# Both attentions of a decoder kernel: scores formed twice, by rows for the maximum and transposed for the exponential

## The chip, the cores and the metric

One program on one NeuronCore of a Trainium2 chip. It runs eight stages one after the other. The metric is the device time of the whole program in microseconds (us); a change under 0.2% is within what repeated measurements of one kernel spread.

## The reference, cut to what matters

Batch 32, sequence 128, width 128, everything float32. The two stages in question compute, for 16 heads of width 8:

```
stage 1 (attn0):  xn = layer_norm(x);  q, k, v = xn @ Wqkv + b;  q, k = rope(q), rope(k)
                  p = softmax(q k^T / sqrt(8) + causal mask);  y = x + (p v) @ Wo + b
stage 4 (attn1):  xn = rms_norm(x);    q, k, v = xn @ wq, wk, wv      (no bias, no rope, no mask)
                  p = softmax(q k^T / sqrt(8));  y = x + (p v) @ wo
```

The other stages are a gelu network, a retention layer, a mixture of experts, a bidirectional Mamba block, a cross attention and a quantized network. They are not changed.

## The kernel before, in words

Each stage is a block of five instruction streams (PE, DVE, ACT, POOL, SP) that run in their own order and meet at semaphores. `attention(..., rope)` at L250 serves both stages; `rope` is true for the first. It takes the 32 batches in groups of G = 4 for the norm and one by one for everything else, as a pipeline written out by hand: in step b each engine works on several batches at once.

In step b, PE (L398) forms the scores of batch b for all 16 heads (L359, into four PSUM banks `ps_s`, with the mask added by a matrix product with the causal table, L355), projects q, k, v of batch b+2 (L406) and the output of batch b-3 (L404), turns attU of b-2 back (L394), turns the probabilities of b-1 (L344), the split q and k of b+1 (L374), and multiplies probabilities with values (L386). DVE finds the maximum of each row (L519) and subtracts it, PSUM to SBUF (L521), divides (L527, L529), takes projections out of PSUM and does the norm (L127 to L155). ACT takes the exponential of `prob` in SBUF (L455) and copies each turned tile out of PSUM (L437, L451, L443). POOL rotates q and k (L495 to L499) and splits them.

Float32 accuracy from bfloat16 products comes from a split: each number is written as a sum of three bfloat16 parts (first, rest, second, third), and the 8 columns of a head are laid out as 7 slots of 8 for q against 7 slots for k (`Parts`, L158), so that one product over 56 rows sums the cross terms. Two heads stand in rows 0 to 55 and 64 to 119 of `qT` and `kT`. No data of these stages goes through DRAM, and SP has only the loads of the weights.

Of the kernel before, what the change touches and what calls it, by code (L numbers as in the profile page):

```python
# [7 lines left out]
ALU = mybir.AluOpType  # L8
# [7 lines left out]
G = 4  # L16
NG = B // G
# [232 lines left out]
def attention(nc, stage, x_all, y_all, c, p, rope):  # L250


    with ExitStack() as stack:
        m = Mem(nc, stack, stage)
        w_qkv = m.sb("w_qkv", [D, 3 * D])
# [4 lines left out]
        xnT = m.sb("xnT", [D, T])  # L260
        qk = m.sb("qk", [T, 2, 2 * D])
        parts = Parts(m)


        v_wide = m.sb("v_wide", [T, G, NJ, NK, 128])
        prob = m.sb("prob", [T, 2, NJ, NK, T])
        probT = m.sb("probT", [T, 2, NJ, NK, T])
        top = m.sb("top", [T, 2, NJ, NK])
        attU = m.sb("attU", [128, NK, T])
        inv = m.sb("inv", [T, 2, H])  # L270
        att = m.sb("att", [T, 2, D])
        attT = m.sb("attT", [D, T])
        if rope:
            b_qkv = m.sb("b_qkv", [T, 3 * D])
            b_o = m.sb("b_o", [T, D])
            cos = m.sb("cos", [T, 2 * D])
            sin = m.sb("sin", [T, 2 * D])
            raw = m.sb("raw", [T, 2, 2 * D])
            turned = m.sb("turned", [T, 2, 2 * D])
        ps_s = m.ps("ps_s", [T, NJ, NK, T])  # L280
        ps_t = m.ps("ps_t", [T, 2, BANK])
        ps_a = m.ps("ps_a", [T, BANK])
        ps_o = m.ps("ps_o", [T, BANK])

        loaded = m.sem("loaded")
        padded = m.sem("padded")
        xn_ready = m.sem("xn_ready")
        turned_in = m.sem("turned_in")
        turned_copied = m.sem("turned_copied")
        proj_ready = m.sem("proj_ready")  # L290
        proj_taken = m.sem("proj_taken")
        qk_ready = m.sem("qk_ready")
        whole_ready = m.sem("whole_ready") if rope else proj_taken
        turn_filled = m.sem("turn_filled")
        turn_taken = m.sem("turn_taken")
        scores_ready = m.sem("scores_ready")
        shifted = m.sem("shifted")
        exp_ready = m.sem("exp_ready")
        pv_ready = m.sem("pv_ready")
        attU_ready = m.sem("attU_ready")  # L300
        attU_turned = m.sem("attU_turned")
        zeroed = m.sem("zeroed")
        att_ready = m.sem("att_ready")
        dve_steps = m.sem("dve_steps")
        pool_steps = m.sem("pool_steps")

        block = stack.enter_context(nc.Block())

        def fills_before(i, b):


            if isinstance(i, int):
                n = i * G + b
                return 2 * max(0, min(n + 1, B)) + NJ * min(max(n - 1, 0), B)
            return i * (G * (2 + NJ)) + 2 * (b + 1) + NJ * (b - 1)

        @block.sync
        def _(sp):
            n = 0
            for dst, src in p["loads"](w_qkv, w_o, gain):
                sp.dma_start(dst, src).then_inc(loaded, 16)
                n += 1
            if rope:
                for dst, src in ((b_qkv[:], all_rows(p["b_qkv"])), (b_o[:], all_rows(p["b_o"])),
                                 (cos[:], p["cos"]), (sin[:], p["sin"])):
                    sp.dma_start(dst, src).then_inc(loaded, 16)  # L330
                    n += 1
            assert n == p["n_loads"]

# [3 lines left out]
        def _(pe):  # L337
            pe.wait_ge(loaded, ALL_LOADED)

            def turn(n, bank, blocks):  # L340

                pe.wait_ge(turn_taken, n + 1)
# [2471 lines left out]
```

## Time and profile before

| | |
|---|---|
| median of 3 runs | 3115.19 us (3112.12 to 3117.36) |
| the profiled execution, its own time | 3120.25 us |
| its span | 3118.4 us, mean granted clock 0.874 |
| busy over the span | PE 73%, DVE 71%, ACT 50%, POOL 46% |
| first attention | about 12.6 to 347.4 us |
| second attention | about 764.2 to 1113.9 us |

Busy time is that of an engine's instructions; the span is from first to last instruction of the profiled execution. Idle time before a group of instructions is put down to the instruction that released it. PE works on float32 with two matrix instructions for one product, so the trace counts twice as many. The granted clock is TensorE's, as a share of 2.4 GHz; its two levels are 1.2 and 2.4 GHz.

### The profile page before, as it was taken

What the parts mean: (1) busy time and instruction counts of PE and PEld (TensorE: products, weight loads), DVE (VectorE), ACT (ScalarE), POOL (GpSimd) and SP (SyncE); (2) the same over time, 40 slices, a digit from 0 to 9 for tenths busy, and PEclk for the clock granted to TensorE, in tenths of its full rate; (3) what the DMA queues carried; (4) which work ended last, traced back from release to release, by engine and by line L of the source; (5) the groups of instructions that cost most, each with busy time, mean ns of one, the idle gap of its engine ahead of it and who ended that gap; (6) DMA issues with size and microseconds to landing.
All of it is one profiled execution on the core that took longest, in us unless ns stands there. A gap on an engine that the chain in (4) does not pass through costs nothing. (4 is left out here: it accounts for less than half of the span.)

```text
span 3118.4 us, 50789 instructions
## 1 busy us (share of the span) xinstructions
PE 2283.5 (73%) x20075; PEld 1444.1 (46%) x20075; DVE 2203.4 (71%) x3826; ACT 1555.6 (50%) x2527; POOL 1421.3 (46%) x1127
## 2 busy tenths in 40 slices
PE   4888666664777769899968989988989975552703
PEld 3555444552555535555534545545545543342303
DVE  4887646885677735555527888888888784888698
ACT  4888515552777732222226666665665651221460
POOL 4555334555222200000007988888988983332001
PEclk9999877886889989999979999999999987665856
DMA  1000010000000010000022222222221220000000
GB/s 40 1 2 2 8 32 18 17 15 4 1 1 1 1 46 1 1 1 1 1 58 59 84 72 69 79 73 68 86 73 63 81 69 24 21 14 8 0 0 27
DMA packets 109916, 95.52 MB, mean 31 GB/s; under 512 B 12256, under 2 KB 106352, under 8 KB 109552
## 3 DMA queue, kind: packets, MB, share of 16 engines
q1 hardware_dynamic: 109680, 92.26, 9.8%
q8 instruction: 162, 2.65, 0.4%
q14 instruction: 74, 0.61, 0.1%
HBM read 83.32 MB, written 2.62 MB: 28 GB/s over the span
## 5 line engine op out<-in xcount | busy, mean ns | idle before, releaser
L1939 POOL TENSOR_TENSOR mam_h<-mam_h,mam_c_all 128x1024 f32<-128x1024 f32 x256 | 644.3, 2529 | 99.3 <-DVE mam_h L2011 98.9
L2011 DVE TENSOR_TENSOR_SCAN mam_h<-mam_decay,mam_ps_b 128x1024 f32<-128x1024 f32 x256 | 574.2, 2275 | 142.5 <-PE mam_ps_b L1642 141.2
L1642 PEld LDWEIGHTS mam_ps_b<-mam_diag,mam_duT 64*128 64x128 f32 x4096 | 250.0, 190 | 252.5 <-DVE mam_h L2011 158.4
L1642 PE MATMUL mam_ps_b<-mam_diag,mam_duT 64*128 64x128 f32 x4096 | 293.3, 286 | 92.4 <-DVE mam_h L2011 80.9
L1833 ACT ACTIVATE mam_decay<-mam_delta,mam_a_neg 128x508 f32<-128x508 f32 x512 | 330.7, 711 | 35.7 <-DVE mam_h L2011 35.5
L1661 PE MATMUL mam_ps_y<-mam_h,all_ident 64*64 64x512 f32 x2048 | 262.5, 629 | 10.0 <-POOL mam_h L1939 10.0
L519 DVE TENSOR_REDUCE at_top<-at_ps_s 128x4 f32<-128x512 f32 x256 | 175.0, 684 | 125.9 <-PE at_ps_s L359 125.9
L1234 ACT ACTIVATE moe_silu<-moe_ps_g 128x512 f32<-128x512 f32 x144 | 86.1, 598 | 289.1 <-PE moe_ps_g L1181 263.0
L437 ACT COPY at_probT<-at_ps_t 128x512 f32<-128x512 f32 x256 | 145.3, 588 | 125.0 <-PE at_ps_t L344 124.7
L198 POOL TENSOR_TENSOR at_parts_rest<-at_qk,at_parts 128x256 f32<-128x256 f32 x64 | 42.9, 671 | 327.7 <-ACT at_parts L193 327.7
L1184 PE MATMUL moe_ps_u<-moe_ynT,moe_w_up 128*128 128x512 f32 x288 | 159.0, 635 | 36.0 <-DVE moe_hidden L1317 36.0
L521 DVE TENSOR_TENSOR at_prob<-at_ps_s,at_top 128x512 f32<-128x512 f32 x256 | 177.1, 692 | 8.8
L1915 POOL TENSOR_TENSOR mam_diag<-mam_halves,mam_b_col 128x512 f32<-128x512 f32 x128 | 149.4, 1168 | 40.8 <-ACT mam_b_col L1807 40.8
L1317 DVE TENSOR_TENSOR moe_hidden<-moe_silu,moe_ps_u 128x512 f32<-128x512 f32 x144 | 97.0, 686 | 99.3 <-PE moe_ps_u L1184 96.4
L344 PE MATMUL at_ps_t<-all_ident,at_prob 128*128 128x128 f32 x1024 | 152.5, 294 | 18.3 <-ACT at_probT L437 17.5
L455 ACT ACTIVATE at_prob<-at_prob 128x512 f32<-128x512 f32 x256 | 159.1, 655 | 4.4 <-DVE at_prob L521 4.3
L1181 PE MATMUL moe_ps_g<-moe_ynT,moe_w_gate 128*128 128x512 f32 x288 | 156.0, 625 | 0.8 <-ACT moe_ynT L1226 0.8
L1194 PEld LDWEIGHTS moe_ps_d<-moe_w_down,moe_hidden 128*128 128x128 f32 x1152 | 140.0, 193 | 32.5 <-issue 32.5
L2277 POOL TENSOR_TENSOR xat_e<-xat_e,xat_inv 128x2048 f32<-128x2048 f32 x16 | 72.1, 4506 | 171.8 <-DVE xat_inv L2299 171.8
L344 PEld LDWEIGHTS at_ps_t<-all_ident,at_prob 128*128 128x128 f32 x1024 | 125.2, 153 | 40.0 <-issue 36.2
L1661 PEld LDWEIGHTS mam_ps_y<-mam_h,all_ident 64*64 64x64 f32 x2048 | 71.6, 138 | 149.1 <-issue 147.2
L1194 PE MATMUL moe_ps_d<-moe_w_down,moe_hidden 128*128 128x128 f32 x1152 | 139.7, 276 | 0.0
(348 smaller groups left out, 4957.2 us busy)
## 6 DMA issues: line engine op xcount, KB each, us to landing
mam_c_all<-mam_c_rows SPq DMA_DIRECT2D x256, 256.0 KB, 3.4
all_x_all<-in_x SPq DMA_DIRECT2D x8, 256.0 KB, 4.6
ret_xg<-all_x_all SPq DMA_DIRECT2D x32, 64.0 KB, 1.8
ret_ctx<-in_ctx SPq DMA_DIRECT2D x32, 64.0 KB, 2.1
mam_xg<-all_x_all SPq DMA_DIRECT2D x8, 256.0 KB, 4.1
xat_xg<-all_x_all SPq DMA_DIRECT2D x8, 256.0 KB, 2.4
xat_ctx<-in_ctx SPq DMA_DIRECT2D x8, 256.0 KB, 3.1
out<-qua_res SPq DMA_DIRECT2D x8, 256.0 KB, 2.3
```

What stands on the lines that cost most here:

```text
L344: last = nc.tensor.matmul(ps_t[:, bank, k * T:(k + 1) * T], blocks(k), c.ident[:], is_transpose=True, start=(k == 0), stop=(k == 3), skip_ ...
L455: nc.scalar.activation(prob[:, b % 2, k, :, :], prob[:, b % 2, k, :, :], ACT.Exp, scale=HD ** -0.5).then_inc(exp_ready, 1)
L519: steps.then(nc.vector.tensor_reduce(top[:, b % 2, j, :], src, AX_X, ALU.max))
L521: nc.vector.tensor_tensor(prob[:, b % 2, j, :, :], src, spread(top[:, b % 2, j, :], T), ALU.subtract)\
L1181: nc.tensor.matmul(ps_g[:, k, :], w_gate[:, e, k * 128:(k + 1) * 128], ynT[:], start=True, stop=True).then_inc(gate_ready, 1)
L1184: last = nc.tensor.matmul(ps_u[:, k, :], w_up[:, e, k * 128:(k + 1) * 128], ynT[:], start=True, stop=True)
L1194: last = nc.tensor.matmul(ps_d[:, o % 2, b, :], hidden[:, o % 2, k, b * T:(b + 1) * T], w_down[:, e, k, :], start=(k == 0 and b == 0), sto ...
L1642: last = nc.tensor.matmul(ps_b[:, slot, odd, :, at // 2, x:x + HT], duT[r, d, s % DT, at, :], diag[r, chunk % SLOTS, at, :, :], start=True ...
L1661: last = nc.tensor.matmul(ps_y[t * HT:(t + 1) * HT, r, :], c.ident[rows, rows], h[rows, (s + t) % H_SLOTS, :, n, :, :].rearrange("p o g t ...
L1833: last = nc.scalar.activation(decay[:, s % SLOTS, :, n, :, 1:T], src, ACT.Exp, scale=a_neg[:, d, s % DT, st:st + 1])
L1939: nc.gpsimd.tensor_tensor(flat(h[:, slot, :, :, :, :]), flat(h[:, slot, :, :, :, :]), flat(c_all[:, chunk, :, :, :, :]), ALU.mult).then_in ...
L2011: nc.vector.tensor_tensor_scan(row(h[:, s % H_SLOTS, :, :, :, :]), row(decay[:, s % SLOTS, :, :, :, :]), row(ps_b[:, s % 2, :, :, :, :]), ...
```

## The change

Both attentions are rewritten. The other stages stay.

- q and k are projected for a whole group of four batches at once, with the weights as the stationary operand, so that they come out already transposed (features down the partitions, 512 columns). With rope there is a second product with the columns of the weights turned by half a head, and DVE multiplies the two with cosine and sine (`turn_half`), POOL adds them (`add_halves`). ACT, POOL, ACT, POOL then make the three parts (`split_first`, `split_rest`, `split_second`, `split_third`), 512 columns each.
- The arrangement in slots is made by DMA through DRAM: SP writes the parts of a group (`write_split`, 2 DMAs each for q and k) and reads them back as rows of 8 KB into `q64` and `k64`, 6 slots of 8 rows for each half (`read_rows`, 6 DMAs for q and 12 for k). The first scores of a group wait for both.
- The scores are formed twice. Once by rows, in `ps_s` (now two banks, half the heads at a time): DVE takes only the maximum over them (`find_top`, 1024 columns). POOL splits the maxima in three (`split_top`), PE turns them with a minus sign (`turn_top`), ACT copies them, SP writes and reads them through DRAM (`write_top`, `read_top`) into three more rows of `q64`, against rows of ones in `k64`. Three steps later (LAG_E) the scores are formed transposed in `ps_e`, over 51 rows, which subtracts the maximum in the same product, and ACT takes the exponential straight from PSUM, 1024 columns at a time.
- Gone are the subtraction on DVE, the turning of the probabilities with its copies, and the turning of the parts with its copies.
- Output projection, v, and the two transposes are done per group as well.

All engines walk through the same steps s, with n = s // 4 and r = s % 4. The diff, cut to its core (the DVE, ACT and POOL helpers do what their names in the list above say):

```diff
+        LAG_E, LAG_V, LAG_U, LAG_O = 3, 4, 5, 2
+        FIRST, LAST = -G, B + 2 * G
+        RUNS = (((0, 0, 3), (3, 0, 2), (5, 0, 1)), ((0, 0, 1), (1, 0, 1), (2, 0, 1), (3, 1, 1), (4, 1, 1), (5, 2, 1)))
 SP
+            def write_split(n, which):
+                sp.wait_ge(third_ready[which], n + 1)
...
+                for r in range(2):
+                    dst = rows_dram[which, r].rearrange("n d (a t) -> (d a) n t", a=PAIRS)
+                    sp.dma_start(dst, split[r * HALF:(r + 1) * HALF, which, :, :]).then_inc(written[which], 16)
+            def read_rows(n, which):
+                slot = n % 2
+                sp.wait_ge(written[which], 16 * 2 * (n + 1))
...
+                for r in range(2):
+                    rows = (q64, k64)[which][r * HALF:(r + 1) * HALF, slot, :, :].rearrange("p a t -> p (a t)")
+                    for at, first, count in RUNS[which]:
+                        src = rows_dram[which, r, first:first + count].rearrange("n d a -> (n d) a")
+                        sp.dma_start(rows[at * HD:(at + count) * HD, :], src).then_inc(landed[which][slot], 16)
...
+            for s in range(FIRST, LAST + 1):
+                if batch(s - 1):
+                    write_top(s - 1)
+                if r == 1 and come:
+                    write_split(n + 1, 0)
+                if r == 2 and come:
+                    write_split(n + 1, 1)
+                if batch(s - 1):
+                    read_top(s - 1)
+                if r == 2 and come:
+                    read_rows(n + 1, 0)
+                if r == 3 and come:
+                    read_rows(n + 1, 1)
 PE
-                    pe.wait_ge(shifted, (i * G + b) * NJ)
-            def turn_probabilities(i, b, n):
-            def turn_parts(i, b, n):
+            def scores_free(b, x):
+                if x == 0 and b % G == 0:
+                    for which in range(2):
+                        pe.wait_ge(landed[which][slot], 16 * 2 * LANDS[which] * (b // G // 2 + 1))
+                if b > 0 or x > 0:
+                    pe.wait_ge(top_ready, 2 * b + x)
+            def both(s, x):
+                now, then = batch(s), batch(s - LAG_E)
+                if now:
+                    scores_free(s, x)
                     if rope:
+                        masks(s, x, ps_s, c.ident_b, c.causal_b)
+                if then:
+                    exponents_free(s - LAG_E, x)
+                    if rope:
+                        masks(s - LAG_E, x, ps_e, c.causal_b, c.ident_b)
+                if now:
+                    products(s, x, ps_s, q64, k64, SLOTS * HD, s_ready)
+                if then:
+                    products(s - LAG_E, x, ps_e, k64, q64, SLOTS * HD + NS, e_filled)
+            for s in range(FIRST, LAST + 1):
+                if r == 0 and come:
+                    turn_x(n + 1)
+                if r == 1 and come:
+                    project("k", n + 1, NP // 2)
+                    if rope:
+                        project("kr", n + 1, 3)
+                both(s, 0)
+                if r == 0 and come:
+                    project("q", n + 1, 0)
+                    if rope:
+                        project("qr", n + 1, 1)
+                if r == 2 and go:
+                    turn_att(n - LAG_O)
+                if batch(s - LAG_V):
+                    values(s - LAG_V)
+                both(s, 1)
+                if r == 3 and go:
+                    output(n - LAG_O)
+                if r == 3 and come:
+                    values_in(n + 1)
+                if batch(s - LAG_U):
+                    turn_back(s - LAG_U)
+                if batch(s):
+                    turn_top(s)
 ACT
-                            nc.scalar.activation(prob[:, b % 2, k, :, :], prob[:, b % 2, k, :, :], ACT.Exp, scale=HD ** -0.5).then_inc(exp_ready, 1)
+                if r == 0 and come:
+                    copy_x(n + 1)
+                if r == 1 and come and not rope:
+                    copy_compact("k", n + 1, 1)
+                if r in (1, 2) and come:
+                    split_first(n + 1, r - 1)
+                if batch(s - LAG_E):
+                    exponentiate(s - LAG_E, 0)
+                if r == 0 and come and not rope:
+                    copy_compact("q", n + 1, 0)
+                if r == 2 and go:
+                    take(("a", n - LAG_O), lambda src: nc.scalar.copy(attT[:], src))
+                if batch(s - LAG_V):
+                    copy_u(s - LAG_V)
+                if r in (1, 2) and come:
+                    split_second(n + 1, r - 1)
+                if batch(s - LAG_E):
+                    exponentiate(s - LAG_E, 1)
+                if batch(s):
+                    copy_top(s)
 POOL
+                if r in (1, 2) and come:
+                    split_rest(n + 1, r - 1)
+                if rope and come and r in (0, 1):
+                    add_halves(n + 1, r)
+                if r in (1, 2) and come:
+                    split_third(n + 1, r - 1)
+                if batch(s):
+                    split_top(s)
+                if r == 1 and whole(n + 2):
+                    before.root(nc, pool, c, n + 2)
 DVE
-                    nc.vector.tensor_tensor(prob[:, b % 2, j, :, :], src, spread(top[:, b % 2, j, :], T), ALU.subtract)\
+                nc.vector.tensor_reduce(top[:, b % 2, :, NJ * x:NJ * x + NJ], ps_s[:], AX_X, ALU.max).then_inc(top_ready, 1)
+            nc.vector.memset(k64[:], 1.0).then_inc(prepared, 1)
```

## Rows read from the trace of the kernel before

**Rows 1.** Windows: busy time of each engine (instructions), granted clock, DMA share, GB/s.
```profile
44.00:330.00 286.00, 237.54 (x2836) 162.00 (x2835) 224.72 (x540) 235.89 (x452) 149.72 (x277) 0.99 0.01 2
795.00:1100.00 305.00, 230.01 (x2717) 173.75 (x2717) 217.77 (x517) 233.55 (x452) 81.28 (x157) 0.91 0.01 2
```

**Rows 2.** The tile attU in either stage: duration ns min/median/max, first and last start.
```profile
L443 ACT COPY at_attU<-at_ps_o x32: 589/632/643, 59.7 to 343.3; 128x512 f32<-128x512 f32 x32
...
L443 ACT COPY at_attU<-at_ps_o x32: 591/630/638, 807.9 to 1110.4; 128x512 f32<-128x512 f32 x32
```

**Rows 3.** Timeline, the ends of both stages: start us, length, engine and line.
```profile
19.81 1.28 ACT L465 ACT_TABLE_LOAD   x1 [19.81 <-DMA at_sin<-in_rope_sin]
...
39.72 0.61 PE L355 MATMUL at_ps_s<-all_causal_b,all_ident_b 128*128 128x512 bf16 x1 [0.95 <-ACT at_kT L451]
...
347.12 0.29 DVE L549 TENSOR_TENSOR all_y_all<-all_y_all,at_b_o 128x128 f32<-128x128 f32 x1
...
764.16 0.33 SPq L325 DMA_DIRECT2D at_w_qkv<-in_L_ffn_wq  x1
...
788.83 1.04 PE L359 MATMUL at_ps_s<-at_kT,at_qT 56*128 56x128 bf16 x16 [0.95 <-ACT at_kT L451]
...
1113.64 0.29 DVE L546 TENSOR_TENSOR all_y_all<-at_ps_a,all_x_all 128x128 f32<-128x128 f32 x1 [1.33 <-PE at_ps_a L404]
```

**Rows 4.** Timeline of steady steps of both stages, PE and the maximum behind it.
```profile
201.64 0.60 PE L394 MATMUL at_ps_o<-all_ident,at_attU 128*128 128x128 f32 x4
...
206.41 1.08 PE L386 MATMUL at_ps_o<-at_probT,at_v_wide 128*32 128x128 f32 x32
...
207.69 0.60 PE L355 MATMUL at_ps_s<-all_causal_b,all_ident_b 128*128 128x512 bf16 x2
...
208.22 0.40 PE L359 MATMUL at_ps_s<-at_kT,at_qT 56*128 56x128 bf16 x8
...
208.66 0.69 DVE L519 TENSOR_REDUCE at_top<-at_ps_s 128x4 f32<-128x512 f32 x1 [1.26 <-PE at_ps_s L359]
...
906.68 0.62 PE L359 MATMUL at_ps_s<-at_kT,at_qT 56*128 56x128 bf16 x16
```

**Rows 5.** Timeline of PE in the gelu stage, at the full clock.
```profile
381.01 7.13 PE L665 MATMUL gelu_ps_h<-gelu_ynT,gelu_w 128*128 128x512 f32 x16 [0.78 <-DVE gelu_total L742]
...
394.72 5.46 PE L672 MATMUL gelu_ps_y<-gelu_w,gelu_hidden 128*128 128x128 f32 x35
```

**Rows 6.** Groups of instructions by line, all stages: busy us, mean ns, idle before.
```profile
L519 DVE TENSOR_REDUCE at_top<-at_ps_s 128x4 f32<-128x512 f32 x256 | 175.0, 684 | 125.9 <-PE at_ps_s L359 125.9
...
L2293 DVE TENSOR_REDUCE xat_top<-xat_ps_s 128x256 f32<-128x2048 f32 x16 | 36.2, 2260 | 18.2 <-PE xat_ps_s L2166 18.0
...
L1822 ACT ACTIVATE mam_pre<-mam_pre 128x1024 f32<-128x1024 f32 x16 | 16.7, 1042 | 0.0
...
L220 POOL CAST at_parts<-at_parts_rest 128x256 bf16<-128x256 f32 x64 | 25.4, 397 | 11.0 <-POOL at_parts_rest L218 11.0
...
L711 POOL TENSOR_TENSOR gelu_skip<-all_x_all,all_y_all 128x512 f32<-128x512 f32 x8 | 10.2, 1280 | 0.0
...
L178 POOL MEMSET at_parts<- 128x4096 bf16 x2 | 7.0, 3512 | 14.5 <-POOLq L36 14.5
...
L479 POOL MEMSET at_v_wide<- 128x16 f32 x8 | 0.5, 125 | 0.1
```

**Rows 7.** Windows of the cross attention, before and after a standstill of PE.
```profile
2684.00:2689.00 5.00, 0.15 (x4) 0.00 (x0) 4.96 (x3) 0.00 (x0) 4.39 (x1) 0.50 0.00 0
2689.00:2694.00 5.00, 4.84 (x36) 2.78 (x37) 3.02 (x1) 2.50 (x2) 0.11 (x1) 0.50 0.00 0
2694.00:2699.00 5.00, 3.79 (x37) 1.66 (x36) 4.75 (x12) 1.76 (x3) 2.51 (x1) 0.92 0.01 3
```

**Rows 8.** Timeline of SP's queue, two loads one behind the other.
```profile
455.06 0.43 SPq L844 DMA_DIRECT2D ret_b_o<-in_L_xattn_out_b  x1
455.53 0.43 SPq L844 DMA_DIRECT2D ret_cos<-in_xpos_cos  x1
```

**Rows 9.** DMA issues: count, KB each, median us from issue to landing.
```profile
ret_xg<-all_x_all SPq DMA_DIRECT2D x32, 64.0 KB, 1.8
ret_ctx<-in_ctx SPq DMA_DIRECT2D x32, 64.0 KB, 2.1
...
ret_decay<-in_decay SPq DMA_DIRECT2D x1, 1024.0 KB, 5.5
...
mam_c_rows<-mam_bc SPq DMA_DIRECT2D x16, 32.0 KB, 3.3
```

More of the change, by code:

```diff
@@ L259, in attention @@
         xn = m.sb("xn", [T, G, D])
[L260 to L272, printed above, removed]
+        xnT = m.sb("xnT", [D, GT])
@@ L290, in attention @@
[L290 to L298, printed above, removed]
+        filled = [m.sem(f"filled{bank}") for bank in range(2)]
+        taken = [m.sem(f"taken{bank}") for bank in range(2)]
@@ new lines, in copy_compact, with split_first @@
+            def copy_compact(name, n, which):
+                if n > 0:
+                    act.wait_ge(rest_ready[which], n)
+                take((name, n), lambda src: nc.scalar.copy(compact[:, which, :], src))
+            def split_first(n, which):
+                if rope:
+                    act.wait_ge(compact_ready[which], n + 1)
+                else:
+                    bank, at = AT[("qk"[which], n)]
+                    act.wait_ge(taken[bank], at + 1)
+                if n > 0:
+                    act.wait_ge(written[which], 16 * 2 * n)
+                nc.scalar.copy(split[:, which, 0, :], compact[:, which, :]).then_inc(first_ready[which], 1)
@@ L506, in _, with add_halves, split_rest @@
-            all_steps(pool, 2, step, 0)
+            def add_halves(n, which):
+                for name in ("qk"[which], "qk"[which] + "r"):
+                    bank, at = AT[(name, n)]
+                    pool.wait_ge(taken[bank], at + 1)
+                nc.gpsimd.tensor_tensor(compact[:, which, :], straight[:, which, :], turned[:, which, :], ALU.add).then_inc(compact_ready[which], 1)
+            def split_rest(n, which):
+                pool.wait_ge(first_ready[which], n + 1)
+                nc.gpsimd.tensor_tensor(rest[:, which, :], compact[:, which, :], split[:, which, 0, :], ALU.subtract).then_inc(rest_ready[which], 1)
@@ L589, in _, with norm @@
-            for b in range(G + 3):
-                step(steps, NG - 1, b)
+            dve.wait_ge(prepared, PREPARED)
+            def norm(n, part):
+                x = x_all[:, n * G:(n + 1) * G, :]
+                if part == 0:
+                    before.take_moments(nc, steps, x)
+                else:
+                    if n > 0:
+                        bank, at = AT[("x", n - 1)]
+                        dve.wait_ge(filled[bank], at + 1)
+                    before.apply(nc, dve, x, lambda b: xn[:, b, :], n, xn_ready)
@@ L593 @@
+            bank, at = AT[("o", NG - 1)]
+            dve.wait_ge(taken[bank], at + 1)
 U = 2
```

556 lines of the change are left out of this document (325 added, 231 removed).

## The prediction

> **What bounds the kernel now.** I read the profile from the page down to single steps. The page's slices show no engine full anywhere in the two attention stages; so the order of the work sets their time, not one engine. The windows say it for their steady parts [rows 1]: in 286 us of the first attention PE is busy 83%, ACT 82%, DVE 79% at a granted clock of 0.99; in the second 75%, 77% and 71% at 0.91. The tile view of attU gives the pace [rows 2]: 31 batches from 59.7 to 343.3 us, 9.15 us each, and from 807.9 to 1110.4, 9.76 each. The timeline gives the ends [rows 3]: the first stage's scores start at 39.7 and its last addition ends at 347.4; the second loads from 764.2, scores from 788.8, ends at 1113.9. A batch goes round scores (PE), maximum and subtraction (DVE), exponential (ACT), turning (PE), copy (ACT), values (PE), and each waits for the one before it.
>
> The other six stages are not touched. I sum the two stages alone and add the difference. Profiled execution: span 3118.4, own time 3120.25; median of the runs shown 3115.19, 5.1 below it.
>
> **Unit costs.** On PE [rows 4]: two 512-column masks 0.53 (207.69 to 208.22); eight products 0.33 with a tail of 0.2 before DVE can start; values 1.0; four transposes 0.55; a float product of 512 columns 0.89 (16 instructions, two each, in 7.13) and of 128 columns 0.31 [rows 5]. DVE and the rest [rows 6]: the maximum over 512 columns took 0.68 and over 2048 2.26, so over 1024 about 1.21. An exponential over 1024 straight from PSUM is not in the trace: 1.04 from SBUF is its lower end, two copies out of PSUM at 0.63 [rows 2] its upper; I take 1.07. POOL: 1.28 over 512 columns; on 16 columns 0.13, and 0.17 between dependent ones (11.0/64). Split_top, four of these, is 1.1 with its entry.
>
> **What goes.** Per batch 16 turned probability blocks, 16 turned parts, four subtractions on DVE (2.7 us at the maximum's 0.68), and on ACT four copies of 512 columns and two of 1024 (2.5 + 2.1 by [rows 2, 6]). **What comes.** A second set of 16 products (and masks in the first stage), the maximum split on POOL and turned, and the round trip through DRAM. Sums for one batch of the first stage, a group's work divided by four: PE 3.45 both sets, 1.0 values, 0.65 turns, and per group four projections 3.6, v and output 1.25 each, x and att 0.55 each, 7.2/4: 6.9. DVE two maxima 2.4, division 0.6, and per group seven passes over 512 columns at 0.68 with norm and v in small pieces, at most 8/4: 5.0. ACT two exponentials 2.15, attU 0.63, top 0.3, and six copies of 512 columns, 3.8/4: 4.0. POOL 1.1 and per group seven operations over 512 columns and the root, 10/4: 3.6. In the second stage PE has 4.3, the others no more than 4.5. All are under the 9.15 and 9.76 of today; so engines are not the bound, two chains are.
>
> **Chain 1, within a step.** PE's turn_top(s) waits for the maxima of its own step, and the next step's scores stand behind it in PE's order. First stage: scores filled 1.6 after the start, maximum 1.21, so the second half starts at 2.85 (values hide under this), filled at 4.45, maximum to 5.7, POOL to 6.9, turn_top to 7.05. Second stage the same with 0.5 for 1.6: 4.9. Projections add to it at r=0 and r=1: two of 0.89 each time in the first stage, one in the second; output and v (2.5) at r=3 fall mostly into that wait of 1.8. Rotation on DVE, the sums and splits of q on POOL and the copies on ACT lie beside PE's work; without that cover q's half alone would add 1.3 a group on POOL, which it does at r=1 of the second stage. If this chain were all, a group of four steps would take 33.1 us in the first stage (8.3 a batch) and 25 in the second (6.3).
>
> **Chain 2, from group to group.** The first scores of a group wait until its k rows have landed; q and k of the next group are projected behind those scores, in the same queue. I follow one group, t=0 where its scores start.
> First stage. r=0: 8.65 by chain 1 with q and qr, and more for the clock. After gaps of 5 us PE ran at 0.50 for about 5 us of work, then near full [rows 7]; PE stands still here for some 8 us before t=0, so +2.5: 11.15. r=1: k and kr 1.8, then the step's 7.05: 8.9. Behind it ACT's in-order queue has copy_top, so only then, counted from the start of r=2, split_first(k) to +1.0; POOL has the root and then rest, to +3.4; second(k) stands behind exponential, att copy and attU copy, to +4.8; third to +6.15. k is split at 26.2.
> Second stage. r=0: 8.1 (5.5, +2.6 for the clock: q and values are no longer hidden). r=1: 7.1, because split_top stands behind third(q) on POOL, and that behind first, rest, exponential, attU copy and second, at +5.9; split_top 1.05. r=2 to third(k): 5.3 (first +1.05, rest +2.4, second behind exponential, att and attU copies +3.95). k is split at 20.5.
> Then SP, alike in both. Each DMA takes its queue 0.475 (455.06 to 455.53 [rows 8]), and waits stand in line: two k writes 1.0, two read_top 1.05, six q reads 2.85, write_top and its landing 1.8 (64 KB landed in 1.8, a 32 KB write to DRAM in 3.3 behind other traffic [rows 9]; 1.8 taken, the SP queue has only just emptied), two read_top 1.05, twelve k reads 5.7, and 1.6 from the end of the last issue to its landing (2.1 from its start, as ret_ctx). 15.05 in all, 25 issues. Nothing hides them: what they wait for is made behind the scores that wait for them. A k read is eight rows of 8 KB; 1 MB in such rows landed in 5.5, which is under 0.46 a row and engine, so bytes keep pace with issues.
> Sum: 41.2 and 35.55. The rest of the clock: PE would be busy two thirds of the first stage's cycle and half of the second's. Rows 1 give 0.99 at 83% and 0.91 at 75%; I take 0.95 (+0.4) and 0.75 (+1.75). **Cycle 41.6 (10.4 a batch) and 37.3 (9.3 a batch).** PE would otherwise be ready at about 35.5 and 29, so it stands still for 6 to 8 us a group.
>
> **The ends.** First stage: loads in at 20.8 (19.8 [rows 3] and two loads more); norm 3.1, x turned and copied 2.0, four projections at half clock 6.9, DVE 0.8, POOL and ACT splitting 5.6, SP and landing 11.05: scores at 50.2 (39.7 now). Seven cycles of 41.6, less 4.5 as group 0 has no values yet, lead to 336.9. Group 7 has no successor to prepare: 4 x 7.05 + 2.5 = 30.7. Drain: six halves of exponential and refill 2.25 each, 13.5, then values, attU, turn back, divide, att, output, additions 9.0: 390.1, against 347.4: **+42.7**. Second stage: setting k64 is not in the trace; POOL's 4096 columns took 3.5 [rows 6], twice that 7.0 (bound below: hidden under the loads at about 4): ready at 771.2, scores at 799.8, seven cycles less 4.0, last group 21.5, drain 18: 1096.4, against 1113.9: **-17.5**. Sum +25, **3140 us** for the median run.
>
> **A rule weighed.** The landing rows run from 1.8 to 5.5 us and grow little with size [rows 9]. The Trainium skill, page "DMA: Bandwidth & Descriptors", section "Anatomy of one DMA", puts about 2.0 us fixed on a DMA, most of it the write receipt and heaviest towards HBM, plus bytes over 436 GB/s. By that the k rows of a group, 786 KB, would cost 3.8 us, not 7.3, and the q rows 1.8, not 2.85; the second rival gives such a result from rows alone.
>
> **Rivals.**
> *Faster, the DRAM chain is shorter than I add up.* Its point: the two cycles make 78.9 us; when they make less than 75.3 (25/7 less), the change wins. For it: the start of a group may keep the full clock (2.5 + 2.6 less), POOL's small operations may take less. Clock kept and landings 0.4 shorter: 7 x 7.2 = 50 less, 3090. Were the wait for rows gone altogether, cycles of 33.1 and 25: 7 x 8.5 + 7 x 12.3 = 146 less, 2994. Against it: 25 issues stand in one queue behind the split of k. Chance 0.25, of it 0.07 for the far end.
> *Faster, bytes and not issues set the reads.* Twelve DMAs overlap: 1 MB landed in 5.5, 1.8 of it fixed; 786 KB in 4.6 in place of 7.3, q 2.0 in place of 2.85: 3.5 less a cycle, 49 in all, 3091. Against it the even 0.475 of [rows 8]. The Trainium skill's rule above would have it so. Chance 0.08.
> *Slower still.* Rows go to 8 partitions and thus to few engines, or the write to DRAM takes the 3.3 of mam_c_rows twice: up to +5 a cycle, 3210. Chance 0.13.
> *No change* (cycles make 75.3 +- 0.9): 0.09. Mine: 0.45.
>
> **Numbers.** A change under 0.2% (6 us) can't be told from none. Range of my own case 3122 to 3180 (a cycle from -1.3 to +2.9). Taking in the near faster cases and most of the slower one: 3060 to 3200. Faster 0.33, same 0.09, slower 0.58.
>
> **What would show it.** In the profile after: DVE's maximum x128 at about 1.21; PE idle before the first scores of each group, released by the DMA of k64, 6 to 8 us; SP's reads in trains of twelve at 0.475; PE waiting at turn_top some 1.8 us a step for POOL; granted clock of the second stage near 0.75; the first stage's end near 390 us, the second's 332 us after its first load (350 now). Wrong if k lands before PE is ready, if reads issue faster, if the reads of k take well over 6 us, or if an exponential from PSUM takes over 1.3.

## The result, and the profile after

3278.37 us (median of 4 runs, 3276.86 to 3287.17) against 3114.49 for the kernel before on the same chip: ratio 1.0531, 95% interval 1.0513 to 1.0549. The change costs 164 us. I had forecast 3140, slower, with 3200 as the upper end: the sign was right, the size far off.

The page of the kernel after: the span, each engine's busy time, and the two groups that replace the maximum and the exponential of [rows 6] (busy, mean ns, idle before and its releaser).

```profile
span 3275.1 us, 48804 instructions
...
PE 2220.7 (68%) x19339; PEld 1353.0 (41%) x19339; DVE 2021.7 (62%) x3246; ACT 1302.8 (40%) x1935; POOL 1330.2 (41%) x1015
...
L739 DVE TENSOR_REDUCE at_top<-at_ps_s 128x8 f32<-128x1024 f32 x128 | 156.8, 1225 | 444.2 <-PE at_ps_s L485 444.1
...
L622 ACT ACTIVATE at_e<-at_ps_e 128x1024 f32<-128x1024 f32 x128 | 131.1, 1024 | 288.7 <-PE at_ps_e L485 288.4
```

The change took the work away that it was to take: DVE is busy 2021.7 us instead of 2203.4, ACT 1302.8 instead of 1555.6. The time went into waiting. The windows of the kernel after over whole cycles of either attention answer to [rows 1] (busy time of PE, PE's weight loads, DVE, ACT and POOL, granted clock, DMA share, GB/s):

```profile
155.00:413.00 258.00, 161.00 (x1702) 89.08 (x1702) 91.14 (x177) 74.03 (x109) 62.57 (x119) 0.76 0.26 49
1000.00:1240.00 240.00, 122.40 (x1666) 85.22 (x1668) 80.75 (x154) 82.67 (x126) 44.80 (x112) 0.71 0.29 55
```

PE is busy 62% and 51%, where it was 83% and 75%, and DVE and ACT about a third. The granted clock fell from 0.99 and 0.91 to 0.76 and 0.71; at the group's start followed below it is 0.50, the lower of its two levels (1.2 GHz). The ends, from the timeline of the kernel after, answer to [rows 3]:

```profile
57.99 1.01 PE L478 MATMUL at_ps_s<-all_causal_b,all_ident_b 128*128 128x512 bf16 x2 [15.00 <-DMA at_k<-at_rows]
...
462.10 1.26 POOL L713 TENSOR_TENSOR all_y_all<-all_y_all,at_b_o 128x512 f32<-128x512 f32 x1 [4.95 <-DVE all_y_all L779]
...
882.64 0.33 SPq L364 DMA_DIRECT2D at_w_qk<-in_L_ffn_wqk  x1
...
924.44 0.61 PE L485 MATMUL at_ps_s<-at_k,at_q 48*128 48x128 bf16 x8 [15.03 <-DMA at_k<-at_rows]
...
1270.19 0.69 DVE L779 TENSOR_TENSOR all_y_all<-at_ps_r,all_x_all 128x512 f32<-128x512 f32 x1 [3.57 <-PE at_ps_r L549]
```

| | before | predicted | after |
|---|---|---|---|
| first attention: first scores, end | 39.7, 347.4 | 50.2, 390.1 | 58.0, 463.4 |
| cycle of a group, mean of seven | 36.6 | 41.6 | 50.6 |
| second attention: load to first scores, length | 24.7, 349.8 | 35.6, 332 | 41.8, 388.2 |
| cycle of a group, mean of seven | 39.0 | 37.3 | 43.5 |

The first attention is 116.0 us longer, the second 38.4, together 154.4 of the 156.7 by which the spans differ. Of the 129 us that the two stages took over the forecast, 106 are in the cycles (7 x 9.0 and 7 x 6.2), 14 in the later first scores (7.8 and 6.2), and some 9 in the last group and the drain.

One cycle of the first attention, SP's queue and PE (kernel after, timeline). The third part of k is done at 182.6:

```profile
155.43 1.01 PE L478 MATMUL at_ps_s<-all_causal_b,all_ident_b 128*128 128x512 bf16 x2 [14.30 <-issue]
...
182.59 1.24 SPq L381 DMA_DIRECT2D at_rows<-at_split  x2
183.87 1.18 SPq L409 DMA_DIRECT2D at_q<-at_tops  x2
185.15 3.49 SPq L393 DMA_DIRECT2D at_q<-at_rows  x6
188.74 0.31 SPq L401 DMA_DIRECT2D at_tops<-at_topT  x1
193.86 0.57 SPq L409 DMA_DIRECT2D at_q<-at_tops  x2
194.53 4.02 SPq L393 DMA_DIRECT2D at_k<-at_rows  x12
198.64 0.31 SPq L401 DMA_DIRECT2D at_tops<-at_topT  x1
...
205.59 1.01 PE L478 MATMUL at_ps_s<-all_causal_b,all_ident_b 128*128 128x512 bf16 x2 [10.43 <-issue]
```

PE's idle time before 205.59 is put down to "issue", that is, to nothing that the profile shows; that it is the landing of k's rows is shown by e1 and e5 below. Such idle time ahead of scores, 169 us in the waits of the kernel after (87.5 + 81.8), is 16.4 in e5.

155.4 to 182.6 is the compute part, 27.2 us (26.2 and 0.4 of clock predicted). 182.6 to 205.6 is SP's part, 23.0 us where I had 15.05. Its issues together are a little quicker than predicted: the twelve reads of k take 4.0 us and not 5.7, the two writes (1.24 for 1.0) and six reads of q (3.5 for 2.85) longer. Two waits for landing are far from the forecast. The maxima, 12 KB written at 188.74, are readable at 193.86: 5.1 us (1.8 predicted). The last read of k is issued at 198.55, and PE starts 7.0 us later (1.6 predicted). Both stand behind rows. (The cycle followed is the mildest of its stage: over the seven, the maxima take 5.1 to 6.8 us, and from the first read of k to the scores it is 11.1 to 12.5.) SP's waits and the windows of the k rows (kernel after; the last columns are clock, DMA share, GB/s):

```profile
SPq L409 <- DMA at_tops<-at_topT: 196.6, 36, 8.1
...
197.00:199.00 2.00, 0.00 (x0) 0.00 (x0) 0.00 (x0) 0.00 (x0) 0.00 (x0) 0.50 0.59 94
199.00:201.00 2.00, 0.00 (x0) 0.00 (x0) 0.00 (x0) 0.00 (x0) 0.00 (x0) 0.50 0.52 85
201.00:203.00 2.00, 0.00 (x0) 0.00 (x0) 0.00 (x0) 0.00 (x0) 0.00 (x0) 0.50 0.52 86
```

No compute engine runs. Of 16 DMA engines 0.52 are busy, 8.3, and they move 85 GB/s: 10.2 GB/s each, 0.80 us for a row of 8 KB. In the kernel before a megabyte in rows of 8 KB landed in 5.5 us [rows 9]. The window of that megabyte shows what one engine did there, 304 GB/s on 0.78 x 16 engines, 24 GB/s each, 0.34 us a row (kernel before):

```profile
458.00:462.00 4.00, 0.00 (x0) 0.00 (x0) 0.00 (x0) 0.00 (x0) 0.10 (x1) 0.50 0.78 304
```

So two things are to be told apart: eight engines instead of sixteen, and a row that takes 0.80 us instead of 0.34.

### The profile page after: what moved, and what is told of

The parts are those of the page before. It is cut to its first block and busy times, and to the rows that moved or that the text cites. A ratio compares the mean times of both kernels' runs of the same rounds, so it can differ in the third digit from the quotient of the medians.

```text
span 3275.1 us, 48804 instructions
## 1 busy us (share of the span) xinstructions
PE 2220.7 (68%) x19339; PEld 1353.0 (41%) x19339; DVE 2021.7 (62%) x3246; ACT 1302.8 (40%) x1935; POOL 1330.2 (41%) x1015
## 5 line engine op out<-in xcount | busy, mean ns | idle before, releaser
L739 DVE TENSOR_REDUCE at_top<-at_ps_s 128x8 f32<-128x1024 f32 x128 | 156.8, 1225 | 444.2 <-PE at_ps_s L485 444.1
L622 ACT ACTIVATE at_e<-at_ps_e 128x1024 f32<-128x1024 f32 x128 | 131.1, 1024 | 288.7 <-PE at_ps_e L485 288.4
L1398 PE MATMUL moe_ps_g<-moe_ynT,moe_w_gate 128*128 128x512 f32 x288 | 156.7, 627 | 0.8 <-ACT moe_ynT L1443 0.8
L687 POOL CAST at_top_split<-at_top 128x16 bf16<-128x16 f32 x64 | 12.7, 198 | 325.2 <-DVE at_top L739 325.2
L485 PE MATMUL at_ps_s<-at_k,at_q 48*128 48x128 bf16 x1024 | 62.7, 256 | 119.1 <-issue 81.8
L1807 PE MATMUL mam_ps_t<-mam_xT,mam_w_tap 128*128 128x512 f32 x256 | 136.0, 660 | 1.2 <-ACT mam_xT L2007 1.2
L478 PE MATMUL at_ps_s<-all_causal_b,all_ident_b 128*128 128x512 bf16 x128 | 46.2, 448 | 108.0 <-issue 87.5
L485 PEld LDWEIGHTS at_ps_s<-at_k,at_q 48*128 48x128 bf16 x1024 | 35.9, 108 | 176.2 <-issue 164.5
```

Of the source, the lines that this page charges most:

```text
L622: nc.scalar.activation(e[:, b % 2, 2 * x:2 * x + 2, :, :].rearrange("p k j t -> p (k j t)"), ps_e[:].rearrange("p r j t -> p (r j t)"), AC ...
L739: nc.vector.tensor_reduce(top[:, b % 2, :, NJ * x:NJ * x + NJ], ps_s[:], AX_X, ALU.max).then_inc(top_ready, 1)
L1398: nc.tensor.matmul(ps_g[:, k, :], w_gate[:, e, k * 128:(k + 1) * 128], ynT[:], start=True, stop=True).then_inc(gate_ready, 1)
L1807: last = nc.tensor.matmul(ps_t[:, bank, :], w_tap[:, d, k, t * 128:(t + 1) * 128], xT[:, d, :, k:k + T], start=(k == 0), stop=(k == W - 1))
```

## The experiments

All ratios are to the kernel before, run on the same chip; the interval is 95%. The cycle is the mean distance of the first maxima of groups in the first attention (seven distances; in e1_stale the last six, since its first still waits for rows). The last two columns are one cycle of its timeline: from the first read of k to the next group's scores, and from the write of a maximum behind q's rows to its reading; blank where it is not given. The profiled execution of e8_lead_late took 3056 us and that of e11_lead_late_lag 3030, both over their medians, so their cycles are a little long.

| run | us | ratio | cycle | k | maxima |
|---|---|---|---|---|---|
| after | 3278 | 1.0531 (1.0513 to 1.0549) | 50.6 | 11.1 | 5.1 |
| e1_stale | 3100 | 0.9936 (0.9915 to 0.9958) | 36.9 | - | - |
| e2_spread | 3278 | 1.0505 (1.0484 to 1.0527) | 49.4 | 9.7 | 2.0 |
| e3_single | 3332 | 1.0692 (1.0658 to 1.0726) | 53.0 | 11.6 | 7.2 |
| e4_merge | 3321 | 1.0644 (1.0622 to 1.0667) | 52.3 | 13.9 | 7.2 |
| e9_by_dim | 3242 | 1.0417 (1.0399 to 1.0434) | 46.9 | 8.8 | 5.3 |
| e7_direct | 3362 | 1.0804 (1.0782 to 1.0825) | 54.8 | 13.7 | 5.8 |
| e6_late | 3213 | 1.0315 (1.0298 to 1.0333) | 45.7 | | |
| e5_lead | 3092 | 0.9935 (0.9919 to 0.9952) | 35.5 | | |
| e8_lead_late | 3045 | 0.9774 (0.9758 to 0.9790) | 30.8 | | |
| e10_lead_late_dim | 3028 | 0.9725 (0.9706 to 0.9744) | 29.9 | | |
| e11_lead_late_lag | 3018 | 0.9694 (0.9677 to 0.9710) | 29.3 | | |
| e12_all | 3005 | 0.9653 (0.9632 to 0.9674) | 28.3 | | |

**e1_stale: no wait for rows after two groups.**

```diff
 def write_split(n, which):
-    if n > 0:
-        sp.wait_ge(landed[which][(n - 1) % 2], 16 * 2 * LANDS[which] * ((n - 1) // 2 + 1))
+    if 0 < n < 3:
+        sp.wait_ge(landed[which][(n - 1) % 2], 16 * 2 * LANDS[which])
 def read_rows(n, which):
+    if n >= 2:
+        return
 def scores_free(b, x):
-    pe.wait_ge(landed[which][slot], 16 * 2 * LANDS[which] * (b // G // 2 + 1))
+    pe.wait_ge(landed[which][slot], 16 * 2 * LANDS[which])
```

> The rows are read back only for the first two groups of four batches; every later group is scored with those (so the scores of later groups are not those of their inputs), while everything is still projected, split and written, and the maxima still go through DRAM. What falls away is the wait of a group's first scores for the rows, and the rows' bytes in the DMA engines. Theory A (the time over the prediction is in the way of the rows through the DMA engines): the cycle from group to group falls from 50.5 us (first attention) and 43.4 (second) to that of the chain inside a step, predicted as 7.05 x 4 + 4.9 and 4.9 x 4 + 5.4, about 33 and 25; that is 6 cycles of 17.5 and 18.4 us less, near 3060 to 3080 us. The landing of the maxima, 5.1 us behind the q rows, falls to about 2. Theory B (the steps themselves are slower than predicted, by the clock or by waits among the engines): the cycles stay above 42 and 35, and the time above 3180 us.

Measured 3100, 178 us less. Theory A in kind, though over its 3060 to 3080: the rows' way is worth more than the whole loss, and SP waits for the written maxima 77.4 us over 36, 2.15 each, in place of 5.46. But the cycles stop at 36.9 and 29.5 us, not 33 and 25, so the steps themselves are 4 us a group longer than I had them, and the first attention still ends at 378.1, later than before the change. One step of this run, from maximum to maximum at r=2, took 8.64 us (270.66 to 279.30) where I had 7.05: the values and the turn of att stand between its halves and outlast the maximum that was to hide them (274.78 to 277.7 against 275.9).

**e2_spread and e3_single: the same rows, apart or side by side.** Both read q in 12 transfers of 8 rows; only e2 has the second line.

```diff
-RUNS = (((0, 0, 3), (3, 0, 2), (5, 0, 1)), ...
+RUNS = (((0, 0, 1), (1, 1, 1), (2, 2, 1), (3, 0, 1), (4, 1, 1), (5, 0, 1)), ...
-sp.dma_start(rows[at * HD:(at + count) * HD, :], src)
+sp.dma_start(rows[at:SLOTS * HD:SLOTS, :], src)
```

> A row of part n and dimension d goes to partition 6 d + n of its half in place of 8 n + d, so the eight rows of one transfer land six partitions apart instead of side by side; q is read in 12 transfers of 8 rows like k, instead of 6. Bytes and results are the same. Theory A1 (8 KB rows that land in neighbouring partitions get in each other's way): the time of a row packet falls from 0.76 us towards the 0.31 that 8 KB packets have elsewhere in this program, the 12 transfers of k are then down from 11 us to the 6 that issue and landing take, the maxima behind q land in 3 us instead of 5, and 14 cycles are 5 to 8 us shorter: 3170 to 3210 us. Theory A2 (a transfer of 8 rows runs on 8 DMA engines and each row costs 0.76 us wherever it lands): the rate of k stays at 85 to 94 GB/s, and the time stays within 15 us of the changed kernel's 3278, plus what the third run, which has 12 transfers of q too, shows.

> Only q is read in 12 transfers of 8 rows in place of 6 of 8, 16 and 24 rows; the rows land where they did. It is the control of the run with the rows spread. If the number of DMA engines that a transfer runs on sets the rate (A2), q slows from 175 GB/s and more to about 90, the maxima that stand behind it land some 4 us later, and the time goes up by 14 x 4 us, to 3320 to 3340 us. If issues set the pace, six more of them at 0.3 us cost 14 x 1.8 = 25 us: about 3300. If it is the partitions' neighbourhood alone (A1), 3300 at most.

The edits of the pair differ in place alone: 3278 against 3332, 54 us. The windows over the whole read of k, kernel after first, then e3_single:

```profile
195.00:205.00 10.00, 0.17 (x2) 0.00 (x0) 0.00 (x0) 0.78 (x1) 0.00 (x0) 0.55 0.47 81
```

```profile
206.50:216.50 10.00, 0.00 (x0) 0.00 (x0) 0.00 (x0) 0.00 (x0) 0.00 (x0) 0.50 0.47 81
```

and e2_spread:

```profile
200.50:208.50 8.00, 0.00 (x0) 0.00 (x0) 0.00 (x0) 0.00 (x0) 0.00 (x0) 0.50 0.33 100
```

81 GB/s on 0.47 x 16 engines are 10.8 GB/s each, 0.76 us a row; 100 on 0.33 x 16 are 18.9, 0.43 us. So a row costs nearly twice as much beside its neighbours, as A1 has it. One rival stays in this pair: e2 issues more slowly and has fewer engines at work at a time, which could also make its rows quicker; e9 below speaks to that. And e2 is no faster than the kernel after, where A1 had 3170 to 3210. The timelines say why, e2_spread first:

```profile
188.72 7.82 SPq L393 DMA_DIRECT2D at_q<-at_rows  x12
196.63 0.39 SPq L401 DMA_DIRECT2D at_tops<-at_topT  x1
198.65 0.57 SPq L409 DMA_DIRECT2D at_q<-at_tops  x2
199.32 7.72 SPq L393 DMA_DIRECT2D at_k<-at_rows  x12
```

e3_single:

```profile
194.06 4.07 SPq L393 DMA_DIRECT2D at_q<-at_rows  x12
198.23 0.31 SPq L401 DMA_DIRECT2D at_tops<-at_topT  x1
205.41 0.57 SPq L409 DMA_DIRECT2D at_q<-at_tops  x2
```

Twelve transfers onto partitions six apart hold SP 7.8 us, 0.65 each, onto neighbours 4.1, 0.34 each. The maxima come back in 2.0 instead of 7.2, the reads of k go 11.6 to 9.7 and are now bound by their issue. What the landing gained, the queue took. e3 lost 54 us to the kernel after, inside the 3320 to 3340 that A2 gave (cycles from 50.6 to 53.0, and from 43.5 to 47.1 in the second attention). The windows over q's reads, kernel after and then e3_single, show why: smaller transfers keep fewer engines busy.

```profile
185.00:191.00 6.00, 6.00 (x80) 4.04 (x80) 2.48 (x3) 2.64 (x3) 0.02 (x1) 0.72 0.80 150
```

```profile
194.00:200.00 6.00, 5.80 (x90) 4.36 (x89) 3.66 (x6) 2.62 (x3) 1.25 (x5) 1.00 0.57 114
```

So both are at work: the number of engines that a transfer runs on (A2) and what a row costs beside its neighbours (A1).

The Trainium skill, page "SBUF — State Buffer", section "Door 1: The DMA port swizzle", has four neighbouring partitions share a port and gives 27.2 GB/s for one port. An estimate from that page is 54 GB/s for eight neighbours. The runs agree in direction, neighbours being slower, but not in size: 85 to 94 GB/s were measured in the kernel after, where several transfers can be under way at once.

**e4_merge: k in 3 transfers with a repeated source.**

```diff
-for at, first, count in RUNS[which]:
+for at, first, count in (RUNS[0], ((0, 0, 3), (3, 1, 2), (5, 2, 1)))[which]:
+    if which == 1:
+        one = rows_dram[1, r, first]
+        src = bass.AP(one.tensor, one.offset, [[0, count]] + list(one.ap))
```

> Rows of k that are the same part are read with one transfer that repeats its source: 3 transfers for each half (24, 16 and 8 rows) in place of 6 of 8 rows. Bytes, places and results are the same. A2 (engines a transfer runs on): k goes at 150 to 200 GB/s instead of 85 to 94, its read is over 3 to 5 us sooner, 14 cycles: 3210 to 3240 us. If only the number of issues counted, 6 fewer at 0.3 us: 14 x 1.8 = 25 us, 3253. If the partitions are the limit (A1) and neighbours in 24 rows are no better off than in 8, less than 25 us.

A miss for every theory: slower, 3321, k read in 13.9 us. The window over the read of k (e4_merge):

```profile
204.00:216.20 12.20, 0.00 (x0) 0.00 (x0) 0.00 (x0) 0.00 (x0) 0.00 (x0) 0.50 0.18 65
```

65 GB/s on 0.18 x 16 = 2.9 engines: 22.6 GB/s each, 0.36 us a row, the quickest rows of these runs, on three engines. They land on the same partitions as in the kernel after, so neighbours alone do not make a row slow; in the kernel after some eight engines write at once. The source of a transfer was 3 (or 2) repeats of 8 rows. The Trainium skill, page "DMA: Bandwidth & Descriptors", section "Why a DMA increments its semaphore by 16 and not by 1", lets a DMA use the largest number up to 16 that divides the slowest size of both sides; that is 3 and 2 here and 8 for eight rows, and the shares 0.18 here (2.9 engines) and 0.52 in the kernel after (8.3) agree.

**e9_by_dim: the repeat inside, the dimension outside.** As e4, with the sources

```diff
-src = rows_dram[which, r, first:first + count].rearrange("n d a -> (n d) a")
+src = rows_dram[which, r, first:first + count].rearrange("n d a -> d n a")
-    src = bass.AP(one.tensor, one.offset, [[0, count]] + list(one.ap))
+    src = bass.AP(one.tensor, one.offset, [one.ap[0], [0, count], one.ap[1]])
```

> Rows are laid out by dimension first inside each run of parts (24, 16 and 8 partitions: part n of dimension d on partition 3 d + n, 2 d + n, d), and both q and k are read with three transfers for each half, k with its source repeated. 12 transfers of rows a group instead of 18, bytes the same. The run that merged k's transfers by parts was slower, 3321 us, while its packets were quick (0.39 us in the middle, against 0.78): its repeated source has 3 for its slowest size, and a transfer on 3 engines would explain both. If the number of engines is set by the slowest sizes of both sides, all these run on 8 engines and land three partitions apart, packets take 0.35 to 0.5 us, k is read in 6 to 8 us instead of 11 and the maxima behind q land in 2 to 3 instead of 5: 14 x 6 us less, 3180 to 3210 us. If it is set by the number of rows alone, the merged run was slow for another reason and this one is at 3250 us or above.

3242, 36 us under the kernel after and 79 under e4 (71 by the ratios, as the two ran on different chips): k's bytes and partitions are those of e4, in another order. The layout of q's rows changed with it. The window over k's read (e9_by_dim):

```profile
236.00:242.50 6.50, 0.00 (x0) 0.00 (x0) 0.00 (x0) 0.00 (x0) 0.00 (x0) 0.50 0.47 123
```

The share is that of the kernel after, 0.47 or 7.5 engines, but each moves 16.4 GB/s instead of 10.8. So with as many engines at work, rows that land apart are quicker (0.50 us against 0.76), and e2's gain is not only that of fewer engines. That the repeated source helps k here too is not excluded. Less than the expected 3180 to 3210 all the same: each transfer holds SP 0.64 us (six in 3.8), and the maxima behind q still took 5.3.

**e7_direct: SBUF to SBUF.**

```diff
-    sp.dma_start(dst, split[r * HALF:(r + 1) * HALF, which, :, :]).then_inc(written[which], 16)
...
-    for at, first, count in RUNS[which]:
+    for at, first, count in ONES[which]:      # twelve transfers of 8 rows, for q too
-    src = rows_dram[which, r, first:first + count].rearrange("n d a -> (n d) a")
+    src = split[r * HALF:(r + 1) * HALF, which, first, :]
```

> The split parts go from their partitions straight to the rows of q and k in SBUF, 12 transfers of 64 KB for q and 12 for k a group, each of 1 KB packets onto 8 partitions side by side; the write of the parts to DRAM and the wait for its landing are gone. Rows one group ahead, everything else as in the changed kernel. If packets of 1 KB onto neighbours get in each other's way as 8 KB rows do, all twelve of k still take about 11 us and q's twelve as long as in the run with single transfers of q, and only the writes and their landing go (2.5 to 4 us a cycle) while q's six more transfers cost 4: 3250 to 3310 us. If what slows the rows is their way out of DRAM, k's read takes 6 us instead of 11 and the cycle is 7 to 9 us shorter: 3150 to 3190 us.

3362, slower than the upper end, 3310. Without a way out of DRAM k's read takes 13.7 us instead of 11.1, so nothing here speaks for that way as the limit; since the packets are smaller as well, the run doesn't exclude it by itself, and e2 against e3, with the same reads from DRAM, is the better witness. Its window in q's rows:

```profile
209.00:211.00 2.00, 0.13 (x1) 0.14 (x2) 1.74 (x7) 0.13 (x1) 0.60 (x1) 1.00 0.60 71
```

Packets of 1 KB onto eight neighbours go at 71 GB/s, and every one of the 24 issues costs 0.65 us.

**e6_late and e5_lead: the two chains one at a time.** e6 moves the turn of a batch's maxima behind the next batch's first half; e5 lets everything up to the rows run two groups ahead (three slots).

```diff
 both(s, 0)
+if batch(s - 1):
+    turn_top(s - 1)
...
-if batch(s):
-    turn_top(s)
```

```diff
-come = whole(n + 1)
+come = whole(n + LEAD)        # LEAD = 2, FIRST = -LEAD * G
-slot = b // G % 2
+slot = b // G % 3
```

> The later turn of the maxima alone, with the rows one group ahead as in the changed kernel. By the prediction's own two chains the part of a cycle up to the third part of k holds about three steps of the chain inside a step, so up to 14 cycles of 3 x 1.7 = 5 us may go, 3278 to about 3210. Rival: the maxima are written half a step later, the queue of SP then waits for them ahead of the write of the parts and of the reads of the rows, and what is won goes again: 3260 to 3300 us.

> Projection, splitting, writing and reading of the rows run two groups ahead of the scores instead of one (three slots for the rows of q and k and for v); all bytes, transfers and results stay. Theory A (the changed kernel loses its time because the first scores of a group wait for a way through the DMA engines that is longer than what is left of the group before): the wait goes, the cycles fall to those of the run with two groups' rows only, about 37 and 29.5 us, and the time to 3100 to 3135 us (a later first group, some 10 us a stage, is part of that). Theory D (the rows' bytes in the DMA engines cost the time also when nobody waits for a group, through the maxima that stand behind them): exponentials wait for the maxima instead, cycles of 43 and 36, 3190 us or more.

e6: 3213 where 3210 was worked out; PE's wait for the split maxima fell from 92.0 us to 12.3 (kernel after, then e6_late):

```profile
PE at_ps_r L532 <- POOL at_top_split L693: 92.0, 52, 2.9
```

```profile
PE at_ps_r L534 <- POOL at_top_split L695: 12.3, 24, 1.3
```

e5: 3092, under the expected 3100 to 3135, and 186 us less than the kernel after with every byte, packet and issue still there. The rows cost their time because a group's scores stood behind them. That is the cause of the loss, shown from two sides (e1 without the rows, e5 with them). Against the kernel before, e5's first attention is still 14.7 us longer (ends at 362.1); the second is 303 long instead of 349.8.

**e8, e10, e11, e12: together.** e8 is e5 and e6; e10 adds e9's layout; e11 adds to e8

```diff
-LAG_E, LAG_V, LAG_U, LAG_O = 3, 4, 5, 2
+LAG_E, LAG_V, LAG_U, LAG_O = 4, 5, 6, 2   # and four slots
```

and e12 has all.

> Rows two groups ahead as in the run before it, and TensorE turns the split maxima of a batch only after the first half of the next batch's scores and exponentials, in place of right behind its own second half. With the rows out of the way the chain inside a step is the bound: VectorE's maximum, the four small GpSimd operations (1.06 us) and the wait until TensorE sees them, 1.65 to 1.9 us a step, leave TensorE's path. 64 steps by 1.7 are 109 us less than with the lead alone: 2990 to 3030 us. Rival: another wait inside the step takes the place (the exponentials, for the maxima that come half a step later), and the gain is under 40 us.

> Rows two groups ahead, the maxima turned half a step later, and rows laid out by dimension so that a transfer's rows land apart (all three of the edits that helped alone). In the run without the layout TensorE still stood some 82 us for the maxima that come back behind q and k rows (at_q from at_tops). The layout had cut SPq's wait for a maximum's write from 196.6 to 147.4 us over 36. If those waits shrink in the same ratio or better, 20 to 60 us go: 2985 to 3025 us. Rival: the longer issue of these transfers (0.64 us against 0.34) holds SP as long as the packets did, and the time stays within 15 us of 3045.

> Rows two groups ahead, the maxima turned half a step later, and the exponentials four steps behind the scores instead of three, the values and what follows one step later too (four slots for q, k and v, so that no slot is waited for). It gives the maxima one step, 7 to 8 us, more for their way, and the landings behind q and k rows took 5 to 9. If TensorE's 82 us of waiting for them are on the path, most go and one step more at each stage's end comes on top (2 x 8): 2975 to 3000 us. Rival: with another bound right behind (PE's own work in a step, 6.5 to 7 us with the maxima, at half clock in parts), less than 20 us: 3025 us or above.

> All four edits together: rows two groups ahead, maxima turned later, rows by dimension, exponentials four steps behind. If the maxima's way is all that is left of the DMA's hold, it is the same as the better of the two others within 10 us, 2970 to 2995 us. If the two remove different waits, up to 20 us less than the better one.

e8 gained 47 of the 109 us, and by the profiled executions all of it in the first attention (the second is 302.5 us long, against 303): with the steps shorter, PE waits for the maxima that come back behind rows. The largest such wait in e8_lead_late, and in e10_lead_late_dim:

```profile
PE at_ps_s L488 <- DMA at_q<-at_tops: 60.6, 10, 9.5
```

```profile
PE at_ps_s L491 <- DMA at_q<-at_tops: 44.8, 10, 6.4
```

The layout shortens it (17 us gained, 20 expected at least). The longer lag removes it (27 gained), and a shorter wait for the exponentials takes its place (42.8 us in e11, 26.7 in e12). Both together gain 40: 3005 us, 3.5% under the kernel before, and 13 us less than the better of the two, so they remove partly different waits. e8, e10, e11 and e12 fell short of their expected ranges by 3 to 18 us. The windows of e12_all, first and second attention:

```profile
98.00:245.00 147.00, 131.94 (x1651) 76.47 (x1653) 89.10 (x173) 70.76 (x108) 60.56 (x118) 0.96 0.34 84
862.00:970.00 108.00, 79.82 (x1351) 59.08 (x1351) 62.94 (x110) 61.94 (x97) 30.71 (x88) 0.89 0.31 79
```

In the first attention PE is busy 90% at a clock of 0.96: there an engine is close to being the bound. In the second it is busy 74% at 0.89, and the waits still are.

## Why the prediction failed, point by point

- **Two chains, not an engine, set the pace; the group's scores wait for k: right.** Shown by e1 and e5 (178 and 186 us) and e6 (66 us). Two of the prediction's own signs of being wrong came up: reads that issue faster than 0.475 us (0.34), and reads of k well over 6 us (11.1).
- **Unit costs of the engines: right.** Maximum 1.225 us (1.21), exponential from PSUM 1.024 (1.07), PE's wait at turn_top 92.0/52 = 1.8 (1.8). Compute part to the third part of k 27.2 (26.6 with the clock). The clocks were forecast too high, for the first attention above all: 0.76 and 0.71 measured, 0.95 and 0.75 predicted. PE stood still there for 12.5 us before a group (87.5 us over 7 in the kernel after's waits; 10.4 in the cycle followed) and not for 6 to 8; that the longer standstill is why the clock was lower is argued, not shown.
- **The step that failed: "bytes keep pace with issues".** I took the row from a megabyte spread over 128 partitions and 16 engines and wrote that 1 MB in 5.5 us is under 0.46 a row and engine (5.5 less 1.8 fixed, over 8 rows an engine). That holds for that transfer, and 96 rows over 16 engines would indeed keep pace. Here a transfer has 8 rows, so 8 engines (share 0.52), all onto neighbours (0.80 us a row in the middle of the read; over the whole read 0.76 in e3 and 0.43 when apart, in e2). Twelve such transfers are 12 x 0.80 = 9.6 us of eight engines, against 4.0 of issue. With it fell the two landings behind rows: k's last, 7.0 for 1.6, and the maxima behind q, 5.1 for 1.8. Together +8.7 a cycle; the issues give 0.8 back and the compute part adds 0.6, which makes 8.5; the cycle that I followed had +8.6 over the forecast. At the start the same reads cost 3.7 of the 7.8 us by which first scores were late.
- **The rival "slower still" named this very mechanism** (8 partitions, few engines) and gave it up to 5 us a cycle and 0.13. It measured 6 to 9. The bound above had to come from a computation, not from a feeling: 96 rows of k on 8 engines, at 0.46 to twice that, are 5.5 to 11 us.
- **The rival "bytes and not issues": right that issues are not the limit, wrong in sign.** By the estimate from the Trainium skill, page "DMA: Bandwidth & Descriptors", section "Anatomy of one DMA", k's rows would take 3.8 us; they took 11.1. That section is on DMAs issued by GpSimd, which the prediction did not say, while these are SP's; and its 436 GB/s is, by "Door 1: The DMA port swizzle" of the Trainium skill's page "SBUF — State Buffer", the rate over all 128 partitions.
- **The rate of the steps.** With the wait gone I had cycles of 33.1 and 25 and 2994 us; e1 measured 36.9 and 29.5 and 3100 us, e5 35.5 and 30.5 and 3092 us. This did not show in the result, since PE would have had to wait anyway, but it would have made the faster rival wrong by 100 us.
- **The other half of the late first scores** (4.1 us ahead of the reads of q): 3.0 of them lie before the first projection, which starts at 28.90 where I had 25.9. A table load on ACT, which I had not counted, holds the turned x for 1.3 of these (kernel after):

```profile
26.77 1.28 ACT L595 ACT_TABLE_LOAD   x1 [26.77 <-PE at_ps_r L445]
...
28.90 5.50 PE L453 MATMUL at_ps_r<-at_xnT,at_w_qk 128*128 128x512 f32 x8 [2.21 <-ACT at_xnT L595]
```

- **What stays open:** how much of the steps' 4 us a group is the clock and how much is PE's order.

## What to carry to other kernels

Price a transfer by the engines it can use and by where its rows land, not by bytes or by another transfer's rate: divide GB/s by the busy share times 16 and compare the rate of one engine. Small results that share a queue with bulk rows are as late as the rows, so give them slack in steps, or another place in the order. When a round trip stands between groups, first ask for one group more of lead: it cost a third slot for q, k and v and turned a loss of 5.3% into a gain of 0.65%, that is 186 us. The shorter steps were worth 66 us without it and 47 on top of it, because by then the maxima behind the rows were waited for: after each edit, ask anew which wait ends last.

## What the runs showed of the hardware

- Rows of 8 KB onto partitions side by side, some eight engines at work: 10.0 to 10.8 GB/s for a DMA engine (kernel after, e3); six partitions apart 18.9 (e2); laid out by dimension 16.4 (e9); side by side but on three engines 22.6 (e4); over all 128 partitions 24 (kernel before).
- The same twelve transfers hold SP's queue 0.34 us each onto neighbouring partitions and 0.65 onto strided ones; so do sources with a repeated or third dimension (0.64).
- A 12 KB write to DRAM and its receipt: 2.0 us behind q's rows in e2, where the rows land apart, and 2.15 on average in e1, with almost no rows; 5.1 us and more behind rows onto neighbours (7.2 in e3).
